# The last stage's activation tiles begin 32 bytes past a multiple of 128 bytes instead of 64

## The reference

```python
x = x + layernorm(attn_ref(layernorm(x)))
x = x + layernorm(ffn_ref(layernorm(x)))

def attn_ref(u):
    z = rmsnorm(u, pre_norm_w) @ in_proj_w.T            # 256 -> 768
    x2, x1, v = split(depthwise_conv3(z) + short_b)
    h = sum_s residues * exp(log_poles * t)             # long filter, 16 poles per channel
    y = (causal_conv(x1 * v, h) + x1 * v * D_skip) * x2
    y = y @ out_proj_w.T + u                            # 256 -> 256
    zm = rmsnorm(y, post_norm_w)
    return y + (gelu(zm @ l1_w.T) * (zm @ l2_w.T)) @ l3_w.T     # 256 -> 672 -> 256

def ffn_ref(x):
    # per batch, W1 and W2 get a sum of rank-one parts made of 16 early tokens of x
    h = gelu(x @ W1'.T + b1)                            # 256 -> 1024
    return h @ W2'.T + b2                               # 1024 -> 256
```

## The kernel before, in words

| part | name of its tiles in the profile | stationary operand | moving operand | matmuls |
|---|---|---|---|---|
| `mlp_block`, unit n | `ps_ring<-mt_*,wl_*` | weights wl1, wl2, wrest | turned rows `mt` | 66 |
| `turn_second`, unit n-1 | `ps_rt<-ident,rows` | `rows` | identity | 4, of 128 columns |
| `ffn_up`, unit n-2 | `ps_ring<-xt_*,we_*` | weights we1 | turned rows `xt` | 48 |
| `out_projection`, unit n+1 | `ps_o<-wout_*,yt_*` | turned rows `yt` | weights wout | 12 |
| `mlp_down`, unit n | `ps_m<-wl_*,pt_*` and line 1617 | turned rows `pt`, `pstack` | weights wl3, wstack | 32 |
| `ffn_down`, unit n-2, chunk 0 | `ps_w<-we_*,ht_*` | turned rows `ht` | weights we2 | 24 |
| `turn_scaled`, unit n+1 | `ps_rt<-ident,rows` | `rows` | identity | 4, of 128 columns |
| `ffn_down`, unit n-2, chunk 1 | `ps_w<-we_*,ht_*` | turned rows `ht` | weights we2 | 24 |

## Time and profile before

### The profile page before, as it was taken

One profiled execution on the slowest core, in us unless ns is written; L12 is line 12 of the kernel. 1 busy time (PEld: TensorE's weight loads), 2 busy tenths in 40 slices (PEclk: granted clock), 3 DMA queues, 4 the chain that ended last, 5 costly groups with the idle time before them and its releaser, 6 DMA issues.

```text
span 1075.0 us, 24951 instructions
## 1 busy us (share of the span) xinstructions
PE 1050.8 (98%) x9012; PEld 1008.5 (94%) x9012; DVE 877.8 (82%) x2322; ACT 710.8 (66%) x1589; POOL 299.5 (28%) x575
## 2 busy tenths in 40 slices
PE   8899999999999999999999999999999999999998
PEld 7777888899989999999999999989999999999997
DVE  7999998774788888888887878897888888887776
ACT  7879887764456666666666666656666666666644
POOL 7677775470101112111111111111112111111111
PEclk9999999999999999999999999999999999999999
DMA  3337977986322222233222222432222223222000
GB/s 130 120 117 236 294 216 196 363 318 151 83 66 41 54 57 50 52 52 58 59 60 58 52 51 60 122 96 41 60 51 50 52 53 59 59 58 60 21 21 31
DMA packets 112491, 102.83 MB, mean 96 GB/s; under 512 B 7552, under 2 KB 103744, under 8 KB 112112
## 3 DMA queue, kind: packets, MB, share of 16 engines
q1 hardware_dynamic: 111136, 98.67, 36.2%
q0 software_dynamic: 736, 2.51, 0.6%
q10 hardware_dynamic: 496, 0.05, 0.0%
HBM read 75.75 MB, written 30.70 MB: 99 GB/s over the span
## 4 chain that ended last, share of the span: by engine, by line
PE 67%; DVE 6%; issue 2%; ACT 1%; POOL 0%; POOLq 0%; DVEq 0%; ACTq 0%
PE ps_ring L1551 35%; PE ps_w L1551 16%; PE ps_m L1551 9%; PE ps_o L1551 4%; PE ps_rt L1566 2%; DVE base L1373 1%; PE ps_w L1561 1%; DVE bn L1277 1%; PE ps_m L1617 1%; DVE prod L1320 0%; DVE ht_l L1289 0%; DVE pt_l L1289 0%; POOL sc L1129 0%; ACT rows L1254 0%; DVE yrow L1512 0%
## 5 line engine op out<-in xcount | busy, mean ns | idle before, releaser
L1129 POOL TENSOR_TENSOR sc<-sc,small 128x2 f32<-128x2 f32 x127 | 94.5, 744 | 676.8 <-DVE sc L1501 404.6
L1194 ACT ACTIVATE gate<-ps_ring 128x256 f32<-128x256 f32 x192 | 73.0, 381 | 129.7 <-PE ps_ring L1551 128.9
L1215 ACT ACTIVATE hid<-ps_ring,small 128x256 f32<-128x256 f32 x256 | 112.1, 483 | 24.2 <-PE ps_w L1551 13.4
L1551 PE MATMUL ps_ring<-mt_l,wl_h 128*128 128x256 f32 x640 | 125.5, 277 | 2.6 <-DVE mt_l L1289 2.6
L1551 PE MATMUL ps_ring<-mt_h,wl_h 128*128 128x256 f32 x640 | 125.5, 277 | 1.8 <-DVE prod L1320 1.3
L1551 PE MATMUL ps_ring<-mt_h,wl_l 128*128 128x256 f32 x640 | 124.9, 277 | 0.0
L1289 DVE TENSOR_TENSOR ht_l<-hid,ht_h 128x256 fp32r<-128x256 f32 x256 | 103.1, 423 | 16.5 <-ACT ht_h L1219 10.6
L1551 PE MATMUL ps_ring<-xt_h,we_h 128*128 128x256 f32 x512 | 104.8, 285 | 2.5 <-DVE prod L1320 2.4
L1551 PE MATMUL ps_ring<-xt_h,we_l 128*128 128x256 f32 x512 | 101.3, 279 | 0.0
L1551 PE MATMUL ps_ring<-xt_l,we_h 128*128 128x256 f32 x512 | 101.3, 279 | 0.0
L1320 DVE TENSOR_TENSOR prod<-ps_ring,gate 128x256 f32<-128x256 f32 x192 | 80.7, 420 | 24.2 <-ACT gate L1194 20.6
(11 more groups left out here) (203 smaller groups left out, 2720.2 us busy)
## 6 DMA issues: line engine op xcount, KB each, us to landing
toep_scratch<-taps_scratch SPq DMA_DIRECT2D x26, 512.0 KB, 7.4
toep<-toep_scratch SPq DMA_DIRECT2D x26, 512.0 KB, 8.8
xa<-in_x SPq DMA_DIRECT2D x16, 512.0 KB, 4.9
x_scratch<-x2c SPq DMA_DIRECT2D x16, 512.0 KB, 3.7
x2s<-x_scratch SPq DMA_DIRECT2D x32, 256.0 KB, 6.7
xa_c<-in_x SPq DMA_DIRECT2D x32, 256.0 KB, 2.7
xb_c<-in_x SPq DMA_DIRECT2D x32, 256.0 KB, 2.7
yin<-seq SPq DMA_DIRECT2D x124, 64.0 KB, 5.5
```

Source lines behind the costliest of these rows:

```text
L1129: nc.gpsimd.tensor_tensor(sc[:, to], sc[:, to], neg_half[:, 0, 0:CC], ALU.pow).then_inc(S[done], 1)
L1194: nc.scalar.activation(gate[rows_of, m % 2], ring[m % RING][rows_of, 0], ACT.Gelu_apprx_tanh).then_inc(S["gate_done"], 1)
L1215: nc.scalar.activation(hid[:, m % HIDS], block_of, ACT.Gelu, bias=b1s[:, m:m + 1]).then_inc(S["hid_done"], 1)
L1551: mm = nc.tensor.matmul(out, lhs(a, kk), rhs(b, kk), start=(j == 0), stop=(closed and j == len(todo) - 1))
```

## The change

One constant. The empty tile has 8 float32, 32 bytes, per partition instead of 16, and everything that is allocated after it moves down by 32 bytes. No instruction is added, removed or reordered. The large tiles after it then lie at 32 modulo 128; what is ahead of it, all weights among it, stays where it is.

```diff
     ACT_HIGHS = FB - 2
     RING = 4
-    OFFSET = 16
+    OFFSET = 8
     FIRST_OUT = (14, 5, 3)
```

## The result

The changed kernel takes 1091.74 us (median of 4 executions, 1091.11 to 1092.38) against 1076.72 us (1076.12 to 1076.87): ratio 1.0139, 95% interval 1.0126 to 1.0151. It is 15.0 us slower. The prediction was 1085 us, 8.3 us slower: right in sign, too small by 6.7 us. Its profiled execution took 1092.38 us, 1.8 us more than its span of 1090.6.

The account below looks back on a forecast made before the run. TensorE, never idle in the last stage's steady units, was taken to bound the kernel. 1076.7 us plus 7.8 us for 26 slower mlp_block parts gave 1084.5, stated as 1085 us; range 1069.5 to 1104 us.

Parts of the forecast that it names:

- The bound: Last stage's steady units, 24.54 us each: all TensorE's, so the matmul rate changes kernel time one to one, some 28 units.
- VectorE, ScalarE and the transfers at nothing: Steady unit: their use of moved tiles costs nothing; VectorE has 4.7 us free, ScalarE 8.5 us.
- `mlp_block` loses the lower level: 26 mlp_block parts: inheritance from ffn_down fails, 66 matmuls go from 7.48 to 7.78 us, adding 7.8 us.
- The rest I leave as it is: where one part of the stationary-side ones becomes slow another may become fast.: All parts except mlp_block: slower and faster parts may offset each other, so no time was added.
- Rival 1: All parts of the last stage run at 117.9 ns a matmul: 16.7 us more, 1093.4 us; chance 0.18.
- rival 2: All products at 120.0 ns, distance 32 acting like distance 0: 1107 us, reaching down to 1098; chance 0.14.
- rival 3: ffn_up behind the transposes gets the lower level, saving 0.21 us in each of 25 parts: 1071 us; chance 0.17.
- rivals 4 and 5: Steady unit: matmuls fall towards 110 ns, 1050 us, chance 0.04; or address does not matter, 1076.7 us, chance 0.14.
- If the distance is no longer the same in both roles: Seam from ffn_down to mlp_block: roles equal modulo 128 at 64, unequal at 32, so inheritance was expected to fail.
- The two read ports: TensorE: the skill's rule that weight loads take nothing from the running matmul would mean no effect, 1076.7 us.
- "lock" of load and stream: TensorE: weight load and stream hold a relative timing that sets the 113.4 or 117.9 ns level, kept or lost by whole parts.
- The prediction's estimate from the 109.2 ns: Last stage free of any disturbance, 256 columns at 109.2 ns a matmul: some 28 us less than now.

Follow-up runs that it names:

- e10: Kernel before with only yt, pt, ht and the rest moved to 32 modulo 256 bytes, mt and xt left in place: 1095.13 us, ratio 1.0168.
- e5: Kernel before with only mt and xt moved to 32 modulo 256 bytes, all other turned rows as before: 1082.89 us, ratio 1.0062.
- the sweep: Kernel before plus unread products ahead of the last stage, 24 per distance, moving or stationary operand shifted by 0 to 240 bytes: 1169.64 us, one execution.
- e6: Kernel before with the empty tile left out, giving distance 0 for every product: 1109.0 us, ratio 1.03.
- e9: Kernel before with mt and xt alone moved 128 bytes further, so the distance is 64 modulo 256 for every product: 1082.44 us, ratio 1.0048.
- e1: Kernel before with an empty 96-byte tile ahead of the weights, moving weights and turned rows together, distances unchanged: 1085.42 us, ratio 1.0076.
- e12: Kernel before with only yt and xt moved by 128 bytes, distances of 64 or 192 modulo 256 chosen part by part: 1072.44 us, ratio 0.995.
- e4: Kernel before with the four transposes of turn_second moved from ahead of ffn_up to behind it: 1079.86 us, ratio 1.003.

## Why the prediction was right or wrong

**The bound.** Right: the rate from matmul to matmul passes to the kernel's time one to one. In the first units, up to 327 us, VectorE sets the pace in between and nothing of the change arrives (a piece that starts at 327.18 us before starts at 327.20 after); from then on each steady unit costs 0.53 us.

**VectorE, ScalarE and the transfers at nothing.** Right, 19.86 against 19.81 us a unit.

**`mlp_block` loses the lower level.** Right in what happens, and only in part in its cause. The prediction expected that the handing on from `ffn_down` would fail. e10 shows that `mlp_block` depends on it, since there it loses the level when the part ahead does. But in e5 the part ahead keeps the lower level, 2.76 us, and `mlp_block` has 7.72 us all the same: its own new distance is enough. The term was 26 x 0.30 = 7.8 us and measured 26 x 0.23 = 6.0, since D = 224 runs at 116.8 ns, not at the upper level of the old distance.

**"The rest I leave as it is: where one part of the stationary-side ones becomes slow another may become fast."** This is the step that failed. At D = 32 no part and no run of the sweep came near 113 ns (117.5 to 118.8), so that `out_projection`, `mlp_down` and `ffn_down` went up in every unit: 1.0 + 3.2 + 5.0 = 9.2 us that the sum lacked. I had reasoned from the kernel before, where these parts exchange levels among themselves, and carried the existence of a lower level over to the new distance. What was left was -0.8 us for `ffn_up` and the 1.2 us outside these parts. The forecast's own picture (66 in 7.78 us, 48 in 5.66, a unit of 24.84) thus explains 6.0 of 15.6 us; the measured time lies outside the 1081 to 1089 us of that case, and the wide range held it because of the rivals.

**Rival 1, every part at the upper level, 1093.4 us,** had a chance of 0.18 and is nearest to what took place: no part has the lower level any more, and the time is 1091.7. That the totals agree within 2 us is partly luck. It took the old upper level, 117.9 ns, for all parts, and so put 7.8 us on `mlp_block`, which lost 6.0, and 0.6 on `ffn_up`, which gained 0.8; it had 0.9 us too little on the parts with stationary turned rows (8.3 against 9.2) and nothing outside the parts. Its argument, that nothing shows by which rule a part gets the lower level, was a reason to take it from all of them. Of the others, rival 2 is not this distance (e6 gives it its own), rival 3 asked `ffn_up` at 5.45 and it has 5.61, rivals 4 and 5 are excluded by the steady unit.

**"If the distance is no longer the same in both roles".** This reason was mistaken, since modulo 256 it never was the same: the handing on that works is the one from 64 to 192, and with equal distances of 64 it fails (e9).

**The two read ports.** The prediction set rows 4 and 5 against the Trainium skill's rule that the next weight load takes nothing from the running matmul. The sweep adds that with weights and stream from one tile, and nothing else changed, the rate goes from 113.1 to 120.0 ns with the distance alone. By the page "TensorE: Matmul & The Clock Gate" of the Trainium skill, section "Step-by-step: what each phase is for", I would expect one rate. So for these operands the measurements do not bear the rule out. That it is the two reads that disturb each other, or a "lock" of load and stream as the prediction called it, is not shown: no run has the same matmuls without their weight loads. The prediction's estimate from the 109.2 ns of the same page of the Trainium skill is also a little low: 206 matmuls at 109.2 ns and the transposes make 23.4 us a unit, 1.16 us less than 24.54, where 110 ns gave 1.0; that is some 31 us over the stage and not 28. The lowest that any run showed is 113.1 ns.

**Open.** Why just these distances are slow or quick, whether the period is 256 bytes or a multiple of it, and whether 113.1 ns is a floor. D = 144 also showed 113.1, with one way of entering it; no kernel here uses it. Nor is it shown what throws e1 from one level to the other.

## What to carry to other kernels

When matmuls with a weight load each follow one another without idle time, divide the length of a chain piece by its count and compare parts of the same shape: here they spread from 113 to 120 ns. How much of that can be had depends on the layout; in this kernel it was 3.3% between the worst (1109.0 us, all at D = 0) and the best (1072.4 us, e12), and 0.5% from the kernel before to e12, all by empty tiles of 32 to 128 bytes per partition, without touching an instruction. Work with the difference of the two start addresses modulo 256, sweep it with products that nobody reads, and then look at the seams between parts, because at a distance that has two rates the part ahead decides which one a run gets. And when a change takes a property away from one part, ask of every part that shares it whether it has one left, before the rest is left as it is.

## What the hardware showed that I had not expected

- The rate of 256-column matmuls with 128-column weight loads depends on the difference of their start addresses modulo 256 bytes, from 113.1 ns (64 and 144) over 116.9 (224) to 120.0 (0, 160 and 176), in one sweep.
- At 64 and 192 there are two rates, 113.3 and 117.8 ns, and a run keeps one for 66 matmuls and more. At 64 a run mostly comes down behind transposes (all 26 `ffn_down` of the kernel before, 13 of 26 in e1), at 192 it mostly does not (2 of 26 `ffn_up` before). Where the roles of the tiles change, 192 keeps the level of a 64 ahead of it, and 64 turned a lower level into the upper one (7.78 us instead of 7.48 in e9). In e4 the lower level ended at a matmul that started 40 ns late.
- Costs of address shifts are not additive: the stationary side alone +1.7%, the moving side alone +0.6%, both +1.4%.
- Two layouts with the same differences of address need not have the same time: e1 took 1.0076 times as long as the kernel before, mostly in the last stage (6.2 of 8.0 us), and its executions spread over 6 us.
